# Expert stage of a two-layer decoder: blocks scatter their results to their tokens' rows, expert numbers packed into words, and inputs turned one batch ahead of their routing

## What is computed

```python
scores = sigmoid(xt @ gate.T)
_, sel = top_k(scores + expert_bias, 2)          # 2 of 8 experts for each token
top_scores = take_along_axis(scores, sel, axis=1)
routed = xt[token_idx] * scores_sorted[:, None]  # each token once for each of its experts
xb = routed.astype(bfloat16)
for e in range(8):
    h = silu(xb @ w1e.T) * (xb @ w3e.T)          # 512 -> 256
    oe = h @ w2e.T                               # 256 -> 512
    out_r += where(expert_ids == e, oe, 0)
hs = silu(xt @ shared_w1.T) * (xt @ shared_w3.T)
out = hs @ shared_w2.T
out = out.at[token_idx].add(out_r)               # then x = layernorm(x + out)
```

## Time and profile before

| | |
|---|---|
| median of 3 runs | 2945.8 us |
| time of the profiled execution | 2947.47 us |
| its span in the trace | 2945.7 us |
| PE busy | 2639.9 us (90%) |
| DVE, ACT, POOL busy | 68%, 50%, 41% |
| expert phase, from its first matmul (2674.3) to the end of the span | 271.4 us |

### The profile page before, as it was taken

The page is one execution under the profiler, slowest core; times in us unless marked ns, Lnnn a source line. Parts: engine busy times, 40 slices in busy tenths (PEclk is TensorE's granted clock), DMA queues, the critical chain, the costliest instruction groups (busy, mean ns, idle before and its releaser), DMA issues. The chain is left out here.

```text
span 2945.7 us, 47353 instructions
## 1 busy us (share of the span) xinstructions
PE 2639.9 (90%) x16941; PEld 1760.8 (60%) x16941; DVE 1988.5 (68%) x2542; ACT 1464.4 (50%) x2868; POOL 1199.9 (41%) x1106
## 2 busy tenths in 40 slices
PE   8999899888888888886999899999997889997886
PEld 5666645534444444443999777777775555556653
DVE  4788757689999999966112079999999733333353
ACT  3444413289999998862222166666666311112410
POOL 0000025446666565542222058688888500001304
PEclk9999999989999999997999999999999999997898
DMA  2123513269888887964002221011112271111163
GB/s 97 65 77 116 201 51 100 77 133 168 170 170 163 170 172 162 191 154 159 32 29 74 100 79 45 26 55 58 51 51 94 77 129 36 43 66 58 61 151 118
DMA packets 534873, 296.52 MB, mean 101 GB/s; under 512 B 438160, under 2 KB 482192, under 8 KB 530832
## 3 DMA queue, kind: packets, MB, share of 16 engines
q1 hardware_dynamic: 518720, 260.31, 35.1%
q0 software_dynamic: 15952, 33.56, 4.0%
HBM read 126.43 MB, written 62.78 MB: 64 GB/s over the span
## 5 line engine op out<-in xcount | busy, mean ns | idle before, releaser
L1181 DVE TENSOR_REDUCE xh_top<-xh_seen 128x1 f32<-128x512 f32 (+1 forms) x768 | 631.3, 863 | 46.0 <-PE xh_seen L1083 32.5
L1153 ACT ACTIVATE xh_prob<-xh_sc,xh_bias,xh_scale 128x1024 int16<-128x1024 f32 (+1 forms) x512 | 609.8, 1201 | 69.5 <-PE xh_sc L1083 69.3
L2328 POOL TENSOR_TENSOR ss_state<-ss_du,ss_b_all 128x1024 f32<-128x1024 f32 x128 | 445.7, 3495 | 169.4 <-PE ss_turned L1926 97.8
L1083 PE MATMUL xh_seen<-xh_kT,xh_qT 96*128 96x512 bf16 x1024 | 354.0, 387 | 81.8 <-DVE xh_top L1181 79.8
L2376 DVE TENSOR_TENSOR_SCAN ss_state<-ss_decay,ss_state 128x1024 f32<-128x1024 f32 x128 | 387.3, 3027 | 27.3 <-ACT ss_decay L2178 27.3
L1083 PE MATMUL xh_sc<-xh_kT,xh_qT 96*128 96x512 bf16 x1024 | 309.0, 384 | 1.3 <-ACT xh_prob L1153 1.3
L1207 POOL CAST xh_probT<-xh_pairs 128x2048 int16<-128x2048 uint8 x128 | 241.8, 1889 | 11.3 <-DMA xh_pairs<-xh_prob 2.7
L1083 PEld LDWEIGHTS xh_seen<-xh_kT,xh_qT 96*128 96x128 bf16 x1024 | 89.3, 97 | 242.8 <-DVE xh_top L1181 220.4
L1933 PE MATMUL ss_bank<-ss_xc,hold_w_conv 128*128 128x256 f32 x1024 | 229.3, 379 | 0.7 <-ACT ss_xc L2190 0.7
L2178 ACT ACTIVATE ss_decay<-ss_delta,ss_a 128x255 f32<-128x255 f32 x512 | 210.7, 496 | 0.4
L1933 PEld LDWEIGHTS ss_bank<-ss_xc,hold_w_conv 128*128 128x128 f32 x1024 | 190.0, 189 | 26.4 <-ACT ss_xc L2190 1.1
(11 more groups left out here) (392 smaller groups left out, 4886.5 us busy)
## 6 DMA issues: line engine op xcount, KB each, us to landing
ex_rows_in<-sa_zeros POOLq DMA_DIRECT2D x18, 1024.0 KB, 6.7
ss_b_all<-ss_states SPq DMA_DIRECT2D x8, 2048.0 KB, 7.2
xa_kT<-xp_kT SPq DMA_DIRECT2D x8, 768.0 KB, 5.3
xh_qT<-xa_qT SPq DMA_DIRECT2D x48, 128.0 KB, 3.2
xh_kT<-xa_kT SPq DMA_DIRECT2D x48, 128.0 KB, 3.3
ex_rows_out<-ex_oe SPq DMA_DIRECT2D x23, 256.0 KB, 2.2
sa_x<-in_x SPq DMA_DIRECT2D x8, 512.0 KB, 3.6
sa_y<-in_x SPq DMA_DIRECT2D x8, 512.0 KB, 10.9
```

Of the source, the lines that this page charges most:

```text
L1083: ins = pe.matmul(out[:, c * D:(c + 1) * D], qT[s][:, t * P:(t + 1) * P], kT[s][:, at + c * D:at + (c + 1) * D], start=True, stop=True)
L1153: act.activation(out, scores, ACT.Exp, bias=bias[t % RING][:, :], scale=scale[s][:, t:t + 1], accum_out=total[s][:, half, t:t + 1]).then_i ...
L1181: ins = v.tensor_reduce(top[t % RING][:, k:k + 1], scores[:, 0:n], AX.X, ALU.max)\
L2328: g.tensor_tensor(state[k % RING][:, :, :], du[s][:, :, :], spread(b_all[s][:, k, :], KD), ALU.mult)\
```

## The change

Five things are changed.

1. A second DRAM tensor `names_in` holds for each row of `rows_in` the row in which its result belongs ("name"): token number times 2 plus 0 or 1, or a row that nobody reads, for rows that pad a block. POOL writes the initial names in the first sublayer and, in routing, scatters the names of each batch beside its rows: eight indirect DMAs a batch instead of four.
2. SP loads a block's 256 names after its rows into one of four `name` buffers (`NAMES`). The name load of block j waits until the results of block j - 4 are scattered, since it uses the same buffer. POOL scatters each block's result from `oe` to `results` with two indirect DMAs. The store of SP falls away, and `take(j)` waits for the scatter of block j - 3.
3. The gathers fall away. After the last block SP loads the results of each batch with one plain DMA; the loads of batches 4 to 7 wait until the results of batch n - 4 are added. The stores of the output stand behind them in SP's program.
4. The plan on DVE makes no result places, and packs the 23 expert numbers into three words. PE reads these after the last `expand_shared` and takes each number with a shift and a mask.
5. On PE and ACT the input n + 3 is turned and copied after `route(n + 2)`, ahead of the shared layer n, one batch earlier than before. Input 2 is turned ahead of `expand_shared(0)`. `count_earlier(7)` has a PSUM bank of its own and doesn't wait for `placed` of batch 6. On ACT `front(3)` stands ahead of `scale(1)`.

```diff
@@ experts, SP
+                if j >= NAMES:
+                    sp.wait_ge(oe_sent[(j - NAMES) % 3], 16 * TB * ((j - NAMES) // 3 + 1))
+                sp.dma_start(name[j % NAMES][:, :], names_in[bass.ds(at, S), :].rearrange("(t p) o -> p (t o)", p=P),
+                             allow_slow_non_contiguous=True).then_inc(name_loaded[j % NAMES], 16)
-            for j in range(3):
-                load_rows(j)
-            for j in range(BLOCKS):
-                if j + 3 < BLOCKS:
-                    load_rows(j + 3)
-                sp.wait_ge(oe_ready, ONE + j + 1)
-                sp.dma_start(block_rows(rows_out, j * S), oe[j % 3][:, :, :]).then_inc(oe_stored[j % 3], 16)
+            for j in range(BLOCKS):
+                load_rows(j)
+            for i in range(3):
+                sp.wait_ge(oe_sent[i], 16 * TB * ((BLOCKS - 1 - i) // 3 + 1))
+            for n in range(B):
+                if n >= PAIRS:
+                    sp.wait_ge(y_ps, ONE + n - PAIRS + 1)
+                sp.dma_start(result[n], results[n * 2 * S:(n + 1) * 2 * S, :]
+                             .rearrange("(t p c) d -> p t (c d)", p=P, c=2)).then_inc(got[n % PAIRS], 16)
@@ experts, POOL
+                for i in (0, 1):
+                    for t in range(TB):
+                        g.indirect_dma_start(names_in, bass.IndirectOffsetOnAxis(ap=place[:, n, i, t:t + 1], axis=0),
+                                             names[:, n, i, t:t + 1], None).then_inc(scattered[n % 2], 16)
+            for j in range(BLOCKS):
+                g.wait_ge(name_loaded[j % NAMES], ONE + 16 * (j // NAMES + 1))
+                g.wait_ge(oe_ready, ONE + j + 1)
+                for t in range(TB):
+                    g.indirect_dma_start(results, bass.IndirectOffsetOnAxis(ap=name[j % NAMES][:, t:t + 1], axis=0),
+                                         oe[j % 3][:, t, :], None).then_inc(oe_sent[j % 3], 16)
-            gather(0)
             for n in range(B):
-                if n + 1 < B:
-                    gather(n + 1)
                 inverse_root(g, ln, n)
@@ experts, PE
-                pe.wait_ge(placed, ONE + n)
+                if n < B - 1:
+                    pe.wait_ge(placed, ONE + n)
+                else:
+                    pe.wait_ge(xT_sb, ONE + B)
+            def load_experts():
+                pe.wait_ge(tab_ready, ONE + 1)
+                return [pe.value_load(experts_at[0:1, i:i + 1], min_val=0, max_val=E ** PER_WORD - 1) for i in range(WORDS)]
+            def expert(j):
+                return pe.snap((words[j // PER_WORD] >> (3 * (j % PER_WORD))) & (E - 1), min_val=0, max_val=E - 1)
             pe.wait_ge(s_loaded, ONE + 48)
+            turn_input(2)
             expand_shared(0)
-            turn_input(2)
             pe.wait_ge(made, ONE + 1)
             count_earlier(0)
             route(2)
+            turn_input(3)
             count_earlier(1)
-            turn_input(3)
             route(3)
+            turn_input(4)
             expand_shared(1)
             for n in range(2, B - 2):
                 count_earlier(n)
-                turn_input(n + 2)
                 route(n + 2)
+                if n + 3 < B:
+                    turn_input(n + 3)
                 expand_shared(n)
@@ experts, ACT
+            front(2)
             gate_shared(0)
-            front(2)
             scale(0)
             odds(2)
+            front(3)
             scale(1)
-            front(3)
             odds(3)
+            front(4)
             gate_shared(1)
             for n in range(2, B - 2):
-                front(n + 2)
                 scale(n)
                 odds(n + 2)
+                if n + 3 < B:
+                    front(n + 3)
                 gate_shared(n)
@@ experts, DVE, take(j)
-                    v.wait_ge(oe_stored[j % 3], ONE + 16 * (j // 3))
+                    v.wait_ge(oe_sent[j % 3], 16 * TB * (j // 3))
```

122 lines of the change are left out of this document (57 added, 65 removed).

## The result

The changed kernel takes 2989.8 us (median of 4 runs, 2987.25 to 2992.26), the kernel before 2946.9 us (2944.82 to 2948.53): a ratio of 1.0146, 95% interval 1.0128 to 1.0163, 43 us slower. I had forecast 2959.8, between 2947 and 2970. The direction was right, the size three times too small.

What follows compares the result with a forecast made beforehand. PE was taken to bound the blocks, routing being a relay of PE, ACT and DVE; 7.2 (first blocks) + 4.4 (block loop) + 2.4 (tail) = 14.0 us more gave 2959.8 us, range 2947 to 2970.

Steps and rivals of the forecast that it cites:

- Input 2: Start of routing: PE waits for input 2's load before turning it, so shared layer 0 ends 10.2 us later.
- Up to the third batch: Routing, shared layer 0's end to batch 2: 22.5 us in all, batch 2 begins at 2728.3 instead of 2719.1.
- POOL in routing: Routing from batch 2: POOL full with eight scatters a batch, 10.1 us each; first transposing load 11.5 us later.
- I take the same 1.27: POOL in routing: a scatter of 4-byte names follows the last after 1.27 us, like one of rows.
- What PE gains there is hidden: End of routing: PE's saved waits and register loads gain nothing, since PE idles 18 us ahead of block 0.
- First blocks: Blocks 0 to 2: rows land 3.4 us after issue, PE starts at half clock; `expand(2)` ends 7.2 us later.
- The block loop: Blocks: name load waits for the scatter of j - 4, 13.7 us per four blocks; twenty blocks 68.3 us, 4.4 more.
- gets it in time: Blocks: `take(j)`, waiting for the scatter of j - 3, is not delayed: 7.0 us against 3 x 3.4 + 1.3.
- rival 1: Blocks: the name wait doesn't bind, PE alone sets the pace, 57.2 instead of 68.3 us; total 2948.7; 10 in 100.
- Sum and norm: Tail: DVE waits for batch 0's output store behind batch 7's load; the end comes 2.4 us later than before.
- the third: Blocks: transfers under load land late, 2 us more per chain turn, 10 us in all; 2969.8; 18 in 100.

Runs made afterwards that it cites:

- a_turn2: The changed kernel with turn_input(2) put back behind expand_shared(0); 2988.7 us, ratio 1.0151 to the kernel before.
- a_names16: The changed kernel with names_in 16 words wide, so name scatters write 64 B elements 64 B apart; 2971.7 us, ratio 1.0092.
- b_both: The kernel before with only the new order of routing (input 2 still behind the shared layer 0) and the packed expert numbers; 2929.6 us, ratio 0.9950.
- w_free: The changed kernel with names 64 B apart, a name buffer for each block and five `oe` buffers instead of three; 2948.7 us, repeated 2950.4 us.
- a_names128: The changed kernel with names_in 128 words wide, so name scatters write 512 B elements 512 B apart; 2974.1 us, ratio 1.0098.
- a_again: The changed kernel itself, run once more for a second profile; 2994.0 us, ratio 1.0162.
- a_names8: The changed kernel with eight name buffers instead of four; 2993.2 us, ratio 1.0169.
- w_stores: The changed kernel with names 64 B apart and output stores 0 to 3 issued between result loads 4 to 7; 2961.4 us, ratio 1.0057.
- b_order: The kernel before with only the new order of routing, expert numbers loaded one by one as before; 2933.5 us, ratio 0.9959.
- the two mended versions: Changed kernel, name buffer per block, five `oe` buffers, stores moved, turn 2 back; names 64 B apart: 2975.4 us; names carried in the rows' scatters: 2941.0 us.

## Why the prediction was too small

By its own steps:

- *Input 2.* Forecast 10.2 us at the end of the shared layer 0, measured 8.1: the wait came (7.7 us), but the shared layer ran in 8.1 us instead of 9.5. **Right**, and of no consequence: a_turn2 shows no difference in the total that its noise allows to tell (1.1 us less by median, 1.5 more by ratio).
- *Up to the third batch.* Forecast +9.2, measured +5.4 us. The queue on ACT was right, and so was its length: `route(3)` began 7.85 us behind the end of the shared layer 0, forecast 7.9. Of the 3.8 us, 2.1 were won before, and the shared layer 1 took 7.8 us where I had up to 9.8.
- *POOL in routing.* This step failed. "I take the same 1.27" was right for POOL (0.96 and 0.30 us to the digit), and with names 64 B apart POOL is full as forecast and the load comes 7.2 us late, 118.1 where I had 122.3. What the step lacked was the landing of the names. I left them at the 2.4 us of the rows; they take 7.2, and 19.6 in the first batch, and the rows behind them 5.5. By the steps of the prediction POOL would have begun batch 2 6.1 us behind the shared layer 1, 56.3 us behind the first turn; it began at 67.7, because `scale(2)` waited for names of batch 0: 11.4 us. From there to its last scatter it took 62.1 us, forecast 59.7, and from that to the first transposing load 6.9 us instead of 2.55, of which 6.8 are the landing of the last names. That is 18.2 us, less the 3.8 that PE was early: the 14.4 us between 122.3 and 136.7. The step had 11.5 us and 25.9 were measured. In a_names16 the load comes 18.6 us sooner, and the total is 18.1 us shorter (15.9 by the ratios). I had a warning of late landings, weighed it as a rival for transfers in the blocks, and didn't work out what it does to the two waits in routing that ask for names to have landed, `scale(n)` and the first transposing load.
- *What PE gains there is hidden.* **Right** in the changed kernel: PE waited 20.6 us ahead of block 0 (forecast 18). The gain itself is 13 to 15 us (b_both) as soon as POOL has only the rows to scatter.
- *First blocks.* From the first transposing load to the end of `expand(2)` 13.1 us, forecast 13.3: **right**.
- *The block loop.* Its mechanism was right and its size was not: a chain of four blocks, with the name load waiting for the scatter of j - 4, forecast at 13.7 us, measured at 16.4 (81.8 us for 20 blocks, forecast 68.3, before 63.9). Terms that were too small, in the first turn of the chain: the landing of the rows 4.2 us instead of 3.4 (3.7 in the median of the blocks, 5.1 at most, against 3.3 before), and `expand` behind the wait 3.56 us instead of 2.0, because it ran at a granted clock of 0.53 behind 3.5 us of idle PE; the mean of the blocks is 0.88. I had taken the clock as full behind each gap of 2 to 3 us. w_free bears the chain out: without the two waits the blocks take 70.6 us, and 20 of them 58.5, close to the 57.2 that rival 1 gives to PE alone. That `take(j)` "gets it in time" held in the changed kernel (0.6 us of idle DVE ahead of it in the blocks).
- *Sum and norm.* Forecast +2.4, measured +4.1 us in the tail (the store landed 5.1 us after issue, not 3.2) and -1.4 from the last `expand` to R. That the tail would be 5 us shorter than before without the wait was right (39.9 and 41.6 against 45.2).
- *Not in the prediction at all:* the end of the span, +3.7 us.

The phase is 31.7 us longer than forecast: 14.2 stand at the end of `expand(2)`, 13.5 come in the block loop, 1.7 in the tail, 3.7 at the end, and 1.4 are won ahead of R. The stages ahead of it, 5.4 us shorter in this execution, take some of that back in the span. The rival that was nearest was the third, transfers that land late, to which I had given 18 in 100 and 10 us. Late landings were what the prediction lacked, but the rival looked for them in the blocks, from a load on the DMA engines, which w_free speaks against. They came in routing, from the names, and their price should have been worked out there.

What is shown: the late landing of 4-byte names side by side (a_names16, a_names128, a_again), the name wait in the blocks (SP's waits in the changed kernel, a_names8, w_free), the store order (w_stores), the gain of the new order (b_order, b_both). What is only argued: how the 2.7 us of each turn in the blocks divide over landing and clock, which I read from one trace. Open: size or distance of the small elements; whether three `oe` buffers would bind once the name wait is gone; what makes engines stand still on some chips, and with it what the two mended versions are worth; why the end of the span grows.

## What to carry to other kernels

A new DMA has two prices, the time of the queue that issues it and the time until it has landed; write both down for each wait that names its semaphore, above all where elements are much smaller than any in the trace. A buffer ring that is released by a scatter puts that scatter's whole latency between two loads of an in-order queue: count the chain with PE at its lower clock behind the wait. A run that is slower than expected should be held against one with the same code on another chip before its program is blamed. A change of several parts should be taken apart: here one part won 13 us and the rest cost some 60 on top of it (2929.6 against 2989.8).

## What the runs showed of the hardware

- Scatters of 128 elements land after 7.2 us (median; 19.6 at most) with 4 B elements 4 B apart, after 2.1 us with 64 B, 2.2 us with 512 B, and 2.4 us with rows of 1 KB (medians; of the 4 B ones half were recorded). POOL issues each in 0.96 us with 0.30 between two.
- Scatters of rows queued behind slow ones land late too, 5.5 us instead of 2.4.
- The end of the program grew with the number of indirect DMAs that POOL had issued in the phase: 9.8 us with 64, 11.0 with 78, 12.4 with 96, 13.6 with 110, some 0.08 us each, in the last barrier, where SP waits for PE's sequencer. Why, no trace shows.
- PE ran an `expand` of 16 matmuls in 1.9 us in the flow (granted clock 1.00) and in 3.56 us behind a wait of 3.5 us (0.53).
- The same routing code ran on one chip with 22 and 25 waits of PE that nothing visible ends, 26 and 32 us in all, and in three runs on other chips with none.
